# Spreading the cross-attention queries of a decoder layer: 16 small transfers per tile inside SBUF in place of two writes to HBM and four reads

## What is computed

```python
x = x + attn(layernorm(x))            # 32 heads of 64 over 8 key heads, RoPE, causal, window of 32
x = x + xattn(layernorm(x), ctx)      # 16 heads of 16, keys and values from ctx (4, 1601, 64)
x = x + ffn(layernorm(x))             # silu(x @ w_gate) * (x @ w_up), 1024 wide, 2:4 sparsified, @ w_down

# xattn
qp = q @ Wq.T                                       # 256 channels = 16 heads x 16
k, v = split(latent_kv @ Wkv_expand.T)
scores = einsum('bhqd,bhkd->bhqk', qh, kh) / sqrt(16)
scores = where(tril(ones(256, 1601)), scores, min)  # so only the first 256 keys count
out = einsum('bhqk,bhkd->bhqd', softmax(scores), vh)
x_attn = out @ Wout.T
```

## Time and profile before

| what | value |
|---|---|
| time, median of 3 runs (lowest, highest) | 428.37 us (427.19, 429.01) |
| profiled execution: its own time | 427.2 us |
| profiled execution: span of its instructions | 425.4 us |
| mean granted clock of TensorE in it | 0.992 |
| busy share of TensorE, VectorE, ScalarE, GpSimd | 94%, 67%, 48%, 38% |
| mean traffic with HBM over the span | 57 GB/s |

### The profile page before, as it was taken

One profiled execution on the slowest core, in us unless ns is written; L12 is line 12 of the kernel. 1 busy time (PEld: TensorE's weight loads), 2 busy tenths in 40 slices (PEclk: granted clock), 3 DMA queues, 4 the chain that ended last, 5 costly groups with the idle time before them and its releaser, 6 DMA issues.

```text
span 425.4 us, 8031 instructions
## 1 busy us (share of the span) xinstructions
PE 399.5 (94%) x2982; PEld 323.0 (76%) x2982; DVE 286.6 (67%) x610; ACT 206.1 (48%) x531; POOL 160.3 (38%) x160
## 2 busy tenths in 40 slices
PE   9997999899899999999899999999989998988996
PEld 8666778668698777877598877877788876756795
DVE  4977931779768971788758992678847993256263
ACT  1364731577325731577335642287435552188330
POOL 4552780388311420368410430267610340047000
PEclk9999999999999999999989999999989999999999
DMA  7975431330002201242001300242000400230000
GB/s 219 362 275 145 124 102 51 106 86 2 2 2 90 67 2 35 70 125 64 2 0 57 99 2 2 99 113 58 0 2 0 150 2 2 74 102 0 2 2 25
DMA packets 33446, 28.90 MB, mean 68 GB/s; under 512 B 18688, under 2 KB 28032, under 8 KB 33152
## 3 DMA queue, kind: packets, MB, share of 16 engines
q1 hardware_dynamic: 33408, 28.40, 21.4%
HBM read 19.21 MB, written 5.24 MB: 57 GB/s over the span
## 4 chain that ended last, share of the span: by engine, by line
PE 75%; DVE 10%; ACT 6%; issue 4%; POOL 3%; DMA 1%; SPq 0%; POOLq 0%; DVEq 0%; ACTq 0%
PE ps L565 13%; PE ps L440 12%; PE ps L629 11%; PE ps L508 7%; PE ps L645 5%; PE ps L471 5%; ACT prob L1169 3%; PE ps L529 3%; PE ps L448 3%; PE ps L551 3%; DVE rope L832 3%; PE ps L604 2%; POOL prob L1062 2%; PE ps L490 1%; PE ps L430 1%
## 5 line engine op out<-in xcount | busy, mean ns | idle before, releaser
L1062 POOL TENSOR_TENSOR prob<-prob,inv 128x512 f32<-128x512 f32 x80 | 83.4, 1048 | 98.4 <-DVE inv L880 98.2
L440 PE MATMUL ps<-xnT,wqk_sb 128*128 128x256 f32 x320 | 79.1, 389 | 0.5 <-DVE rope L832 0.4
L440 PEld LDWEIGHTS ps<-xnT,wqk_sb 128*128 128x128 f32 x320 | 58.0, 191 | 12.4 <-issue 6.1
L1169 ACT ACTIVATE prob<-ps,mx 128x128 f32<-128x128 f32 (+1 forms) x128 | 53.0, 434 | 15.3 <-DVE mx L858 12.1
L1055 POOL TENSOR_TENSOR qs<-rope 128x512 f32<-128x512 f32 x32 | 40.8, 1274 | 43.9 <-DVE rope L832 41.2
L1179 ACT ACTIVATE pT<-ps 128x512 f32<-128x512 f32 x80 | 48.0, 604 | 14.2 <-PE ps L508 13.7
L508 PE MATMUL ps<-ident_sb,prob 128*128 128x128 f32 x320 | 48.9, 277 | 3.7 <-POOL prob L1062 3.7
L832 DVE TENSOR_TENSOR rope<-ps,trig_sb 64x512 f32<-64x512 f32 x74 | 50.9, 688 | 1.0
L508 PEld LDWEIGHTS ps<-ident_sb,prob 128*128 128x128 f32 x320 | 36.9, 140 | 11.4 <-POOL prob L1062 6.8
L858 DVE TENSOR_REDUCE mx<-ps 128x2 f32<-128x512 f32 (+1 forms) x48 | 32.7, 689 | 12.6 <-PE ps L490 12.0
L1041 POOL TENSOR_TENSOR rstd<-vareps,power 128x1 f32<-128x1 f32 x24 | 13.1, 550 | 74.1 <-DVE vareps L811 73.9
(11 more groups left out here) (124 smaller groups left out, 692.3 us busy)
## 6 DMA issues: line engine op xcount, KB each, us to landing
k<-kx SPq DMA_DIRECT2D x32, 128.0 KB, 2.9
q<-qx SPq DMA_DIRECT2D x32, 128.0 KB, 2.6
vb<-v_sb SPq DMA_DIRECT2D x42, 64.0 KB, 2.1
wqk_sb<-in_wqk SPq DMA_DIRECT2D x4, 512.0 KB, 7.1
work<-in_wgu SPq DMA_DIRECT2D x4, 512.0 KB, 9.0
wo_sb<-in_wo SPq DMA_DIRECT2D x1, 2048.0 KB, 14.6
vb<-v_sb SPq DMA_DIRECT2D x36, 32.0 KB, 2.2
wd_sb<-in_wd SPq DMA_DIRECT2D x1, 1024.0 KB, 5.5
```

The source lines that it names most:

```text
L440: mm = pe.matmul(o[:, half, :], wqk_sb[:, k, g, half, :], xnT[:, 0, k, :], start=(k == 0), stop=(k == KT - 1))
L1062: pool.tensor_tensor(p, p, inv[:, i % ND, 0:g].unsqueeze(2).broadcast_to([P, g, 512 // g]), ALU.mult).then_inc(s_norm, 1)
L1169: ins = act.activation(prob[:, i % ND, h * k:(h + 1) * k], ps[:, BANK_S + i % 2, h * k:(h + 1) * k], ACT.Exp, bias=mx[:, i % ND, h:h + 1], ...
```

## The change

`cross_queries` on SyncE no longer writes to HBM. It waits for x_hi (`s_q2hi`) and for the space of `q4`, issues eight transfers of the high part, waits until x_lo is written, and issues eight transfers of the low part. Each transfer takes 32 partitions of `q2p`, one row of 1 KB from each, and writes them to every fourth partition of one slot of `q4`. The HBM tensor `qx` and its semaphore go, and TensorE waits for 16 transfers a tile (256) in place of 4 (64). The bytes written to `q4` are the same.

```diff
@@ -247,7 +247,6 @@
         s_kx = sem("s_kx")
         s_k4 = sem("s_k4")
         s_q2hi = sem("s_q2hi")
-        s_qx = sem("s_qx")
         s_q4 = [sem(f"s_q4{t}") for t in range(TT)]
         s_o2T = sem("s_o2T")
         s_mag = sem("s_mag")
@@ -260,7 +259,6 @@
         s_out = sem("s_out")
 
         kx = nc.dram_tensor("kx", (2, P, HG * S), F32, kind="Internal").ap()
-        qx = nc.dram_tensor("qx", (2, TT, P, HG * P), F32, kind="Internal").ap()
 
         def bank(name, b):
             k, _ = ring_use(name, b)
@@ -338,18 +336,19 @@
                                      kx[c // 2].rearrange("(i e d) n -> e d i n", e=2, d=XD)[e]).then_inc(s_k4, 16)
 
             def cross_queries(b, t):
-                n = TT * b + t + 1
-                wait_drained(sp, f"xq{t}", b)
-                for part in range(2):
-                    sp.dma_start(qx[part, t], q2p[part][:, t].bitcast(F32).rearrange("p g n -> p (g n)")).then_inc(s_qx, 16)
-                sp.wait_ge(s_qx, 32 * n)
+
+                sp.wait_ge(s_q2hi, TT * b + t + 1)
                 if b:
                     wait_filled(sp, "down", b - 1)
                 else:
                     sp.wait_ge(s_wlo, WCHUNKS)
-                for c in range(4):
-                    sp.dma_start(q4[c::4, t].bitcast(F32).rearrange("p i g n -> p i (g n)"),
-                                 qx[c % 2, t].rearrange("(i m) n -> m i n", m=2 * XD)).then_inc(s_q4[t], 16)
+                for part in range(2):
+                    if part:
+                        wait_drained(sp, f"xq{t}", b)
+                    for c in (part, part + 2):
+                        for i in range(HPT // 2):
+                            sp.dma_start(q4[c::4, t, i].bitcast(F32),
+                                         q2p[part][32 * i:32 * i + 32, t].bitcast(F32)).then_inc(s_q4[t], 16)
 
             def load_x(b):
                 return x[b].rearrange("(t p) d -> p t d", p=P)
@@ -475,9 +474,9 @@
                     j = i - NQB
                     if j == 0:
                         pe.wait_ge(s_k4, 128 * (b + 1))
-                        pe.wait_ge(s_q4[0], 64 * (b + 1))
+                        pe.wait_ge(s_q4[0], 256 * (b + 1))
                     if j == XU0:
-                        pe.wait_ge(s_q4[1], 64 * (b + 1))
+                        pe.wait_ge(s_q4[1], 256 * (b + 1))
                     tile = 0 if j < XU0 else 1
                     heads = cross_heads(j)
                     n, g, keys = len(heads), heads[0] // HPT, (tile + 1) * P
```

## The result

| | before | after |
|---|---|---|
| median of the runs (lowest, highest) | 428.69 us (427.19, 429.98), 4 runs | 449.69 us (447.62, 451.20), 4 runs |
| ratio, 95% interval | | 1.0493 [1.0448, 1.0538] |
| profiled execution: its own time, span | 427.2, 425.4 us | 447.62, 445.8 us |
| mean granted clock | 0.992 | 0.969 |

What follows compares the result with a forecast made beforehand. TensorE's program order was taken to bound the kernel, with the HBM trip hidden nearly everywhere. Tile 1's delays of 4.2, 3.4, 3.4 and 7.0 us sum to 17.9, giving 446 us (+4.1%), range 434 to 451.

Steps and rivals of the forecast that it cites:

- The bound, and where the slack is read: TensorE, busy 94%, sets the time; slack runs from tile 0's x_hi to each tile's first units, 18.24 us for tile 1, batch 0.
- The price of an issue: On SP's queue, each of the 32-partition transfers costs a pitch of 0.65 us, taken from v_blocks; ends kept 0.37 and 0.67.
- the middle price: Rival on SP's queue: an issue costs the 64-partition pitch of 0.57 us, sum 8 to 9.5 us, 437 us; chance 0.20.
- the plain one: Rival price on SP's queue: a pitch of 0.47 us, as for 128 partitions, so not measurably slower, 430.5 us; chance 0.12.
- the 0.33 and 0.43 rows: Issue times of the old path's two writes per tile from SBUF to HBM, 128 partitions in rows of 1 KB.
- (b): Rival on SP's queue: not slower, issue pitch 0.47 us, sum 2.0 to 2.4 us, 430.5 us; chance 0.12.
- The landing: After a tile's last issue, the transfer lands in 2.1 us, the median of v_blocks; bounds 1.9 and 2.6.
- The sum per batch: At tile 1's first unit, TensorE is late by 4.2, 3.4, 3.4 and 7.0 us in batches 0 to 3, together 17.9.
- The waits at tile 1: At L486, TensorE waits for q at tile 1 about 1.4, 0.6, 0.6 and 2.5 us in batches 0 to 3.
- The clock: Granted clock falling to 0.50 behind tile 0's wait: nothing added to the forecast, 2.5 us kept for the range.
- Costed at nothing: Earlier waits and transfers queued behind on SP: v_blocks begin at 89.7 instead of 83.02, with 38 us of cover.
- The early start: SP issues the high part after x_hi, without waiting for x_lo; losing this would cost 0.4 us a tile.

Runs made afterwards that it cites:

- the 4 transfers: Changed kernel with the same 512 KB per tile in 4 transfers of 128 partitions by 1 KB, spreading left out; 428.37 us, ratio 0.999.
- the early old way: Kernel before, with x_hi sent to HBM as soon as written and read back while x_lo is on its way; 427.94 us, ratio 0.9991.
- The probes: Kernel before plus bursts of five transfers per form on SP's idle queue in batch 3; issues 0.59 to 0.60 us inside SBUF, 0.42 to 0.60 with HBM.

## Why the prediction was right

- **The bound, and where the slack is read.** Right. TensorE's order and the two waits in `unit_scores` set the time; that nothing measurable comes from the trip saved is shown twice, by the 4 transfers (0.999) and by the early old way (0.9991).
- **The price of an issue.** 0.65 us of pitch forecast, 0.63 measured. The row chosen, v_blocks, was the right one, but a part of the argument for it was wrong: the case for the middle price and against the plain one said that fewer partitions cost more. The probes show 0.59 us at any count inside SBUF, and 0.42 at 32 partitions of 1 KB with HBM. What v_blocks share with the new transfers and the 0.33 and 0.43 rows don't is that both sides are SBUF. That isn't the whole rule, since 64 partitions and the reads of `qx` cost 0.60 with HBM on one side; what sets the price there is open. Of the rivals, (b) rested on 128-partition rows to HBM, and the kernel with 4 transfers shows that even 128 partitions don't have that price inside SBUF.
- **The landing.** 2.1 us forecast, 1.9 measured, both small beside 31 pitches.
- **The sum per batch.** 4.2, 3.4, 3.4, 7.0 forecast; 4.2, 3.4, 3.8, 6.3 measured, 17.6 for 17.9. That tile 1's row is late because it stands behind tile 0's on the same queue is shown by the kernel that moves eight issues to ScalarE's; how far the two tiles' delays overlap stays open. The sum's step that TensorE comes to tile 1 a full 2.8 us late in batch 0 was wrong: it is there at 88.38, 19.5 us after x_hi and not 21.0, since its waits for exponentials between the two tiles (1.82, 0.27 and 0.79 us in batch 0 of the kernel before) took up a part. This changed the wait at tile 1 (2.90 us for 1.4) and not its end, which the landing sets.
- **The waits at tile 1.** Eight were forecast and six came. In batches 1 and 2 TensorE reaches tile 1 with the landing, with no wait in the rows: behind tile 0's wait it ran at half clock, which used up the 0.6 us forecast as a wait. With TensorE kept at work the waits are seven, 0.34 and 0.54 us of them at these two places.
- **The clock.** This is the term that was mis-sized. It was put at nothing, with 2.5 us kept for the range; it is 5.1 us by the ratios, with an uncertainty of 2.2. The first profiled execution, of 447.62 us, shows 3.2 us: 2.8 behind tile 1's begin, in batches 0 and 3, and 0.4 in batch 2, where TensorE comes to tile 1 after the landing. The step that failed is that only the fall behind tile 0's wait was counted. The clock also falls behind tile 1's wait, where no later wait hides it. With TensorE kept at work the median is 445.1 us; without it, it is 449.7 and, measured again, 451.4.
- **The range.** It held with some luck. Its upper part was 2.5 us of clock and 2.0 us of a slower landing. The slower landing didn't come, and the clock alone took what was kept for both. The second median, 451.39 us, lies just above the range's 451.
- **Costed at nothing.** v_blocks began at 89.98 (forecast 89.7) and nobody waited for them. The output and the next keys moved alike.
- **The early start** was said to be worth 0.4 us a tile. The trace of the kernel without it shows that delay at tile 0; its time doesn't resolve it.
- **The rules of the Trainium skill.** That many small transfers are to be coalesced (DMA: Bandwidth & Descriptors, Rules for kernel authors) is borne out: 16, 8 and 4 transfers of the same bytes give 449.7, 428.2 and 428.4 us, and what decides is the slack, not the size. That the time to initiate a DMA is usually small relative to the DMA itself (the same page of the Trainium skill, Issuing engines are not separate DMA queues) doesn't hold here: 0.59 us of issue stand against 1.9 to the landing.

## What to carry to other kernels

A trip to HBM that is off the chain is worth nothing when it is taken away, and its replacement has to fit the same slack. Count the issues: n transfers in one row on one queue take n times the price of one, here 0.6 us inside SBUF for any size from 8 to 128 KB, and the next row on the queue starts late by as much. Where a wait of some us on TensorE is new, count what the clock loses behind each such wait, not only behind the first.

## What the runs showed of the hardware

- The price of an issue on SP's queue, the transfers one behind the other: 0.59 to 0.60 us from SBUF to SBUF at 16, 32, 64 and 128 partitions, with or without a stride; with HBM on one side and rows of 1 KB, 0.42 to 0.45 us at 32 and 128 partitions and 0.60 at 64, but 0.60 also for the kernel before's reads of 128 KB into 32 partitions. ScalarE's queue issued transfers of 32 partitions inside SBUF at 0.62 us.
- Two queues issue at the same time without slowing each other by more than the rows vary: 8 issues in 5.07 us on ScalarE's beside 8 in 5.19 us on SP's; SP's alone took 4.92 to 5.47 us.
- TensorE stood still for 2.2 to 3.8 us in the changed kernel's six new waits, and behind each the granted clock fell to 0.50 (1.2 of 2.4 GHz). It doesn't fall behind every such wait: with tile 0 alone by the new way, waits of 2.4 and 2.2 us in batches 0 and 1 were followed by 1.00. Three to eight calls of a matmul without use in each wait kept it at 1.00 and took 5.1 us (by the ratios) off the time.
- A stretch of three slices at 0.50 that nothing hides costs 1.2 to 1.7 us. The cleanest case is the kernel with 4 transfers: batch 2 lasts 100.34 us there and 98.67 before, with the same begin of both tiles and one stretch more, at 358.
- A float32 matmul call of 256 columns shows as two matmuls in the trace, and 20 of them in a row take 4.48 us, 0.22 each, so a filler is to be sized by the trace and not by calls.
